# A ring of gathered rows: GpSimd waits for two free slots at every second group

## The reference

```
Q, K, V = x @ WQ, x @ WK, x @ WV          # N x 128, seen as N x 8 x 16
Eh      = edge_attr @ WE                  # E x 8 x 16
score   = exp(clip(sum_d(K[src] * Q[dst] / 4 * Eh), -5, 5))     # E x 8
wV      = segment_sum(V[src] * score, dst)
Z       = segment_sum(score, dst)
h       = x + wV / (Z + 1e-6)
y       = batch_norm(h) over the nodes, times gamma, plus beta
out     = layer_norm(x + y)
```

## Time and profile before

| | us |
|---|---|
| median of 3 runs | 2175.12 |
| lowest and highest | 2172.72, 2175.36 |
| span of the profiled execution, first to last instruction | 2636.3 |
| POOL busy in it | 1620.7 |
| DVE busy | 1649.3 |
| PE busy | 2052.8 |
| mean granted TensorE clock, share of full speed | 0.618 |

### The profile page before, as it was taken

One profiled execution on the slowest core, in us unless ns is written; L12 is line 12 of the kernel. 1 busy time (PEld: TensorE's weight loads), 2 busy tenths in 40 slices (PEclk: granted clock), 3 DMA queues, 4 the chain that ended last, 5 costly groups with the idle time before them and its releaser, 6 DMA issues.

```text
span 2636.3 us, 43652 instructions
## 1 busy us (share of the span) xinstructions
PE 2052.8 (78%) x12749; PEld 1850.1 (70%) x12749; DVE 1649.3 (63%) x3732; ACT 809.8 (31%) x1876; POOL 1620.7 (61%) x1700
## 2 busy tenths in 40 slices
PE   8787778777778877777877777777777877787786
PEld 7677767766667767666777767776766776676775
DVE  5365666666666666666666666666666666666687
ACT  2332222222323222223223222222232332322335
POOL 7466666666666666666666666666666666666624
PEclk8855665565666556665556566565656656655678
DMA  9555555555555555555555555555555555555553
GB/s 346 180 166 164 176 156 177 169 165 163 169 166 173 166 160 175 168 160 170 170 157 172 178 168 167 162 170 166 174 157 165 172 158 179 166 159 169 173 193 110
DMA packets 190913, 451.93 MB, mean 171 GB/s; under 512 B 91470, under 2 KB 99102, under 8 KB 176800
## 3 DMA queue, kind: packets, MB, share of 16 engines
q1 hardware_dynamic: 111792, 235.81, 27.7%
q0 software_dynamic: 78960, 214.67, 26.6%
HBM read 420.34 MB, written 29.98 MB: 171 GB/s over the span
## 4 chain that ended last, share of the span: by engine, by line
PE 32%; DVE 32%; issue 17%; another core or an unknown queue 13%; DVEq 3%; ACT 1%; POOL 0%; DMA 0%; SPq 0%; POOLq 0%; ACTq 0%
PE eh_ps L839 10%; PE agg_ps L847 10%; DVE kq L1164 7%; DVE ssum L1167 7%; DVE ring L1017 6%; DVE kq L1158 5%; PE qe_ps L829 4%; PE agg_ps L849 4%; DVE onehot L1092 2%; DVEq L1096 2%; PE aux_ps L857 1%; DVE acc L1106 1%; DVE z_live L1107 1%; PE aux_ps L743 1%
## 5 line engine op out<-in xcount | busy, mean ns | idle before, releaser
L562 POOL DMA_INDIRECT ring<-kv_rows,src_t x1613 | 1534.9, 952 | 915.2 <-remote 453.4
L839 PE MATMUL eh_ps<-we_sb,ea 128*128 128x128 f32 x3322 | 809.0, 407 | 297.8 <-issue 193.5
L839 PEld LDWEIGHTS eh_ps<-we_sb,ea 128*128 128x128 f32 x3322 | 696.7, 302 | 341.2 <-issue 226.0
L847 PEld LDWEIGHTS agg_ps<-onehot,ring 128*128 128x128 f32 x3322 | 657.5, 291 | 199.3 <-issue 188.3
L1158 DVE TENSOR_TENSOR kq<-ring,qe_ps 128x512 f32<-128x512 f32 x416 | 285.2, 685 | 790.8 <-remote 592.4
L847 PE MATMUL agg_ps<-onehot,ring 128*128 128x42 f32 x3322 | 662.4, 368 | 136.0 <-issue 100.0
L641 ACT ACTIVATE qe_ps<-sclip 128x32 f32<-128x32 f32 x416 | 83.6, 201 | 1707.2 <-DVE sclip L1169 1049.4
L1164 DVE TENSOR_TENSOR kq<-kq,eh_ps 128x512 f32<-128x512 f32 x416 | 285.7, 687 | 59.5 <-issue 7.9
L635 ACT ACTIVATE ohT<-ohT,ones 126x512 bf16<-126x512 bf16 x416 | 300.1, 721 | 13.5
L633 ACT ACTIVATE ohT<-rel_wide,minus_w 126x512 bf16<-126x512 bf16 x416 | 294.9, 709 | 0.0
L1167 DVE TENSOR_REDUCE ssum<-kq 128x32 f32<-128x512 f32 x416 | 285.0, 685 | 14.3
(11 more groups left out here) (151 smaller groups left out, 857.5 us busy)
## 6 DMA issues: line engine op xcount, KB each, us to landing
ea<-in_edgeT SPq DMA_DIRECT2D x104, 1024.0 KB
rel_wide<-rel_rows SPq DMA_DIRECT2D x104, 512.0 KB
ring<-kv_rows,src_t POOLq DMA_INDIRECT x1613
q_win<-q_rows SPq DMA_DIRECT2D x416, 31.5 KB
kv_rows<-ring SPq DMA_DIRECT2D x24, 512.0 KB
q_rows<-q_st SPq DMA_DIRECT2D x27, 360.0 KB
ring<-in_xT SPq DMA_DIRECT2D x12, 512.0 KB, 5.6
xq<-in_xT SPq DMA_DIRECT2D x25, 240.0 KB
```

Of the source, the lines that this page charges most:

```text
L562: pool.indirect_dma_start(out=kv[:, s, j, :], out_offset=None, in_=kv_rows, in_offset=bass.IndirectOffsetOnAxis(ap=src_t[:, n * TILES + j: ...
L839: last = pe.matmul(eh_ps[s % 2][:, j * P:(j + 1) * P], ea[:, s % EARS, j * P:(j + 1) * P], we_sb[:, :], start=True, stop=True)
L847: pe.matmul(msg_ps[s % 2], kv[:, room_of(s), j, D:KV], onehot[:, s % 8, j, :], start=(j == 0), stop=(j == tiles_of(n) - 1))
```

## The change

The wait for a free slot is made at groups of even number only, and there it is for one group more: before group n (even) the sums of group n-15 must be done, which frees the slots of n-16 and n-15. Group n+1 then has its slot, and POOL issues its four gathers behind those of n with no wait between.

```diff
-                if n >= SLOTS:
-                    pool.wait_ge(agg_ready, n - SLOTS + 1)
+                if n >= SLOTS and n % 2 == 0:
+                    pool.wait_ge(agg_ready, n - SLOTS + 2)
```

## The result

| 20 runs each | median | lowest to highest |
|---|---|---|
| before | 2172.88 us | 2171.18 to 2175.36 |
| after | 2176.36 us | 2173.75 to 2182.47 |

The ratio of the means is 1.0019, 95% interval 1.0013 to 1.0025: the change costs 4.1 us by it and 3.5 us by the medians, forecast 5.0. In later runs the same kernel before took 2172 to 2174 us on two chips and 2600 and 2629 us on two others. Its first profile, with its span of 2636.3 us, is like those of the second kind; which chip it was taken on is not known.

What follows compares the result with a forecast made beforehand. POOL's gathers were taken to bound the timed runs. To the median of 2175.1 us the late start added 5.0 and all other terms 0, giving 2180; range 2167 to 2188, the likeliest case's own 2177 to 2182.

Steps and rivals of the forecast that it cites:

- The sum of POOL alone: Whole timed run: group 16's start at 123.72, 1597 gathers taking 2007 us, 58.7 us after the last group's data; 2190.
- the 461 us: Profiled span of 2636.3 us against the timed median of 2175.12: the excess, 21%.
- what POOL really waits: POOL's idle time before gathers in the first profile, without the issue share: 453.4 + 30.7 = 484 us.
- Item 1: POOL's 200 removed waits: a satisfied wait costs 0, so removing them saves 0, at most 2 us.
- Item 2: Unsatisfied slot waits in the loop: even groups' gathers start up to 6.0 us later, hidden by the 84 us lead; 0.
- Item 3: Loop start: group 16 waits for group 1's sums, not group 0's, delaying each later gather; 5.0 us, between 3.6 and 5.0.
- the cap of 5.00: Start of the loop: group 17 moves from 129.80 to 134.80, limiting the delay to 5.00 us despite signals 6.08 us apart.
- Item 4: Eight gathers in a row beside edge loads: transfers have room, so 0, at most 104 us if nothing hid it.
- A lead that lasts: Timed loop: PE and DVE need near 4.8 us a group, POOL's lead is never eaten up; no change, 2175, chance 0.22.
- Costly waits: Timed loop: unsatisfied waits each cost more than the time to the signal, halving them saves 8 us; 2167, chance 0.13.
- Delayed edge loads: Rows of eight gathers delay edge loads or Q rows until PE waits; 15 us slower, 2190, chance 0.10.
- The signs: Expected in the changed profile: rows of eight, group 16 near 129.8, lead 13 to 14 groups, span 2636 within 1%.

## Why the prediction was right, and where it was not

*What bounds the timed runs.* Right. The sum of POOL alone gave 2190, 15 us over the median. The same sum by the profile after: the start at 110.71, 1597 gathers of 0.948 + 0.305 us, 2001, which makes 2112; DVE's first product on the last group at 2115.20; and 58.8 us from there to the end, 2174.0. The terms for the gathers (2007) and for what follows the last group (58.7) were right to 0.3%; the excess was in the first, 123.7 against 104.8 in the kernel before. I had put it down to profiling, before and behind the loop; behind it there is none (58.7 and 58.8 us), and the start at 123.7 belongs to the other kind of chip.

*Why the profiled execution was longer.* Wrong. I took the 461 us for the cost of profiling. Profiled executions of both kernels take 2174 us, so profiling costs nothing that shows, and the first profile has the marks of a chip of the second kind. The conclusion held, by some luck, because POOL's 1.25 us per gather is the same on both kinds, and because the terms for the gathers and the end do not wait for PE. The 484 us of "what POOL really waits" also hold 253 gaps of 0.30 us; the true waits were 407 us.

*Item 1, satisfied waits cost nothing.* Right, 1200 more of them: 1.0000.

*Item 2, the later request is hidden.* Right where POOL is the bound: no gather after group 16 waits. Wrong for the profiled execution, whose kind of chip I forecast to stay at its time: 31 us slower. The step that failed is the one from "the lead covers the later gathers" to "nothing is lost": the lead stayed, 13 groups, and the time rose all the same.

*Item 3, the start.* Right in mechanism, and it is all of the change: 5.0 forecast, 4.3 to 4.6 by the signals within one trace, 4.6 with that wait alone changed, 4.1 for the change. The signals are not the 6.08 us of the earlier trace rows apart, so it is the signal and not the cap of 5.00 that counts. The size was over by 0.9 us for this reason, and that a cap that plays no part lay so near it was luck.

*Item 4, bursts.* Right where POOL is the bound, by the run with pairs from group 18 on and by the rows of sixteen. The Trainium skill's rule on turns between queues ("DMA: Bandwidth & Descriptors", section "SWDGE vs HWDGE vs iDMA") changed nothing that these runs can see. Not settled for the second kind of chip, where rows of eight came with a loss of 1.2%.

*The rivals.* A lead that lasts: refuted on the first kind of chip, DVE waits for rows (246.3 us), and the lead was gone after some 70 groups, inside the 50 to 150 that were forecast. On the second kind the lead does last, but the time is not unchanged. Costly waits: refuted by the run with 1200 more of them and by the pairs from group 18 on. Delayed edge loads: refuted on the first kind of chip. The bound of 0.2%, 4.35 us, lay inside the forecast's own range, and the result, 0.19%, fell just under it, on the side that had 0.17 against 0.38.

*The signs.* Three of them came out otherwise though the timed forecast held: the span fell to 2174.0, group 16 started at 110.71 and not near 129.8, and at 1237.6 us POOL was one group ahead and not 13 to 14. By the prediction a fallen span would have meant that waits disturb only when profiled; the kernel before, with all its waits and a profiled span of 2173.8 us, refutes that.

## What to carry to other kernels

Where a producer is the bound, it can't make up any idle time. It meets a real wait only early, before its consumers have fallen back on its pace: ask of each coarser wait when its first ones are met, before asking how many are saved. A trace whose span is far from the timed median may be of another regime, so take another before explaining it; check the bound by adding up one engine alone with durations that do not depend on the others. And compare on more than one chip: a change that costs 0.2% on one cost 1.2% on another.

## What was not expected of the hardware

The chips met here fall into two kinds: 2173 us on two and 2600 and 2629 us on two others for one kernel, steady to 0.4% on each, with much the same gather, 0.946 to 0.949 us (median). Each chip was met once, so a lasting property of it is not told apart from a state that it was in at the time. In the first profile, which looks like the slower ones, PE and DVE take 6.00 us a group with gathers under way and 3.48 without; but PE's granted clock is 0.60 in the one stretch and 0.81 in the other, and what of the difference is clock and what is standing still was not separated. On the faster ones a gather's length differs by 3 ns between executions, 949 against 946, also between runs on one chip; over 1597 gathers in a row that is 4.8 us, and would account for the scatter of 4 to 9 us between runs of one kernel. That it does was not measured.
